# Running sums later, the weight sum T1 stored once, one statistics segment per batch, and the last batch's routing moved into the second phase's first rows

## The reference

```python
h = x @ base_weight.T + base_bias + (x @ A.T) @ Bw.T      # A, Bw of the batch's lora id
query = h @ Wq.T                                          # 2048 -> 64
scores = (query @ Wr.T) @ (aux_keys @ Wr.T).T / sqrt(48) + log_rel
top_scores, top_idx = top_k(scores, 8)                    # 8 of 512 slots
attn = einsum(query, aux_keys[top_idx]) / sqrt(64) + log_rel[top_idx]
w = softmax(attn)
aux = (w @ aux_values[top_idx]) @ Wvd.T @ Wvu.T
log_var = log1p(var(h, axis=-1))
learned = gelu(h @ Wu1.T + bu1) @ Wu2.T + bu2             # 2048 -> 512 -> 1
u = clip(0.5 * log_var / mean(log_var) + 2.5 * sigmoid(learned), 0, 5)
gate = sigmoid(0.5 * clip((u - 0.5) / 1.5, 0, 1) - 1.0)   # 0 where below 0.05
out = x + h + gate * aux
```

## Time and profile before

| | |
|---|---|
| median of 3 runs | 1995.03 us (1994.07 to 2000.32) |
| profiled execution | 1995.2 us, span 1993.4 us |
| PE busy | 1943.9 us (98%), mean granted clock 0.989 |
| DVE busy | 1262.0 us (63%) |
| ACT busy | 693.7 us (35%) |
| POOL busy | 400.9 us (20%) |
| DMA | 414.46 MB, mean 208 GB/s |

### The profile page before, as it was taken

The page is one execution under the profiler, slowest core; times in us unless marked ns, Lnnn a source line. Parts: engine busy times, 40 slices in busy tenths (PEclk is TensorE's granted clock), DMA queues, the critical chain, the costliest instruction groups (busy, mean ns, idle before and its releaser), DMA issues.

```text
span 1993.4 us, 24866 instructions
## 1 busy us (share of the span) xinstructions
PE 1943.9 (98%) x8682; PEld 1582.2 (79%) x8682; DVE 1262.0 (63%) x1656; ACT 693.7 (35%) x1051; POOL 400.9 (20%) x283
## 2 busy tenths in 40 slices
PE   8999999999999999999999999999999999999996
PEld 6877877888888888888888877777888888888875
DVE  5775688555467836546873643677377677667666
ACT  3422433333233433324333322344233323332332
POOL 2210122120022202002210100110433323233323
PEclk9989999999999999999999999999999999999997
DMA  7656777552367745146764434757977677777774
GB/s 268 229 190 244 254 252 258 168 173 74 131 202 232 225 147 187 45 154 210 234 208 140 159 106 171 240 184 236 326 269 270 231 244 236 229 241 237 274 275 164
DMA packets 195201, 414.46 MB, mean 208 GB/s; under 512 B 26692, under 2 KB 27716, under 8 KB 194950
## 3 DMA queue, kind: packets, MB, share of 16 engines
q1 hardware_dynamic: 150150, 324.78, 50.3%
q10 hardware_dynamic: 44928, 88.10, 11.5%
HBM read 316.32 MB, written 96.47 MB: 207 GB/s over the span
## 4 chain that ended last, share of the span: by engine, by line
PE 86%; DVE 7%; issue 3%; ACT 2%; DMA 2%; ACTq 0%; SPq 0%; DVEq 0%; POOL 0%; POOLq 0%
PE bank L1659 17%; PE bank L1660 17%; PE bank L1661 17%; PE bank L1697 6%; PE bank L1698 6%; PE bank L1699 6%; PE bank L1712 1%; PE bank L1713 1%; PE bank L1599 1%; PE bank L1600 1%; PE bank L1786 1%; PE bank L1788 1%; PE bank L1787 1%; DVE sums L1261 1%; PE bank L1767 1%
## 5 line engine op out<-in xcount | busy, mean ns | idle before, releaser
L1659 PE MATMUL bank<-xop,wsp 128*128 128x512 f32 x1792 | 710.7, 397 | 14.9 <-DVE wsp L1152 8.0
L1660 PE MATMUL bank<-xop,wsp 128*128 128x512 f32 x1792 | 701.8, 392 | 0.0
L1661 PE MATMUL bank<-xop,wsp 128*128 128x512 f32 x1792 | 700.9, 391 | 0.0
L1659 PEld LDWEIGHTS bank<-xop,wsp 128*128 128x128 f32 x1792 | 338.5, 189 | 98.6 <-DVE xop L1152 8.0
L1660 PEld LDWEIGHTS bank<-xop,wsp 128*128 128x128 f32 x1792 | 338.9, 189 | 74.5 <-issue 3.8
L1661 PEld LDWEIGHTS bank<-xop,wsp 128*128 128x128 f32 x1792 | 338.2, 189 | 72.4
L1152 DVE TENSOR_TENSOR wsp<-wraw,wsp 128x1024 fp32r<-128x1024 f32 x184 | 241.2, 1311 | 122.0 <-ACT wsp L790 121.7
L790 ACT ACTIVATE wsp<-wraw 128x1024 fp32r<-128x1024 f32 x184 | 194.0, 1054 | 204.3 <-PE bank L1661 170.9
L779 POOL TENSOR_TENSOR r_h<-r_h,r_x 128x512 f32<-128x512 f32 x128 | 172.7, 1349 | 363.7 <-DMA r_h<-h_dram 363.7
L877 ACT ACTIVATE stage<-stage 128x512 f32<-128x512 f32 x128 | 80.9, 632 | 406.1 <-DVE stage L1247 405.7
L1261 DVE TENSOR_TENSOR sums<-sums,stage 128x1024 f32<-128x1024 f32 x116 | 154.5, 1332 | 92.2 <-ACT stage L877 92.2
(11 more groups left out here) (158 smaller groups left out, 1957.9 us busy)
## 6 DMA issues: line engine op xcount, KB each, us to landing
wraw<-in_w SPq DMA_DIRECT2D x131, 512.0 KB, 3.8
xraw<-in_x SPq DMA_DIRECT2D x248, 256.0 KB, 4.2
wraw<-t_dram SPq DMA_DIRECT2D x80, 512.0 KB, 3.6
h_dram<-stage ACTq DMA_DIRECT2D x128, 256.0 KB, 3.9
hraw<-h_dram SPq DMA_DIRECT2D x128, 256.0 KB, 4.0
r_x<-in_x SPq DMA_DIRECT2D x128, 256.0 KB, 4.4
r_h<-h_dram SPq DMA_DIRECT2D x128, 256.0 KB, 3.5
out<-o_st ACTq DMA_DIRECT2D x96, 256.0 KB, 3.8
```

The costliest lines, as they stand in the source:

```text
L1659: pe.matmul(ps, wsp[:, slot, 0, f], x_hi(i), start=(k == 0), stop=False)
L1660: pe.matmul(ps, wsp[:, slot, 0, f], x_lo(i), start=False, stop=False)
L1661: last = pe.matmul(ps, wsp[:, slot, 1, f], x_hi(i), start=False, stop=(k == HT - 1))
```

## The change

- `add_sums(g - 2)` stands at the end of the iteration, in front of `finish(g - 1)`.
- The sums are kept per batch: two segments per pair, so 8 passes in place of 12; the last is in step 5 of phase 2. What uses the statistics moves from steps 4 to 9 to steps 7 to 14.
- ACT stores T1 from `t_res` in the iteration after it was made (`store_t1`); T2 waits until that has landed (`t_moved`). `make_t1_again` is gone, and M5 of pair 0 loads T1 from `t_dram` as the other pairs do. T4 is made beside tiles 16 to 23 (18 to 25 before).
- Batch 7 (`EARLY`): in row 0 of phase 2 ACT and DVE split its h from `r_h` before POOL adds x, and PE makes its query there with a lag of two steps. In rows 1 to 4 its four token tiles pass through scores, attention, selection and softmax, one per row in steps 14 and 15 (`SEQ` is the order of all of them). The normalised weights go to `a7_dram` and come back in row 7. At the end only the gate is multiplied in (`gated`).
- Selection has one DVE operation fewer per token tile, for all batches: MATCH_REPLACE writes 1e30, and one operation subtracts it and adds the attention.
- The end: 9 of batch 6's output blocks are added by DVE (`add_last6`), 7 are evacuated by ACT and added by POOL, in the order `TAIL6`; SP's stores of the two batches alternate.

```diff
         T1_AT = dict(zip((1, 2, 3, 4, 5, 6, 9, 11), range(HT)))
         T2_AT = dict(zip((8, 10, 12, 13, 14, 15, 16, 17), range(HT)))
-        T4_AT = {18 + o: o for o in range(HT)}
+        T4_AT = {16 + o: o for o in range(HT)}
         T3_AT = {M7 * HT - 3 + o: o for o in range(HT)}
-        T1B_AT = {M5 * HT - 3 + o: o for o in range(HT)}
...
-            early = p == 0 and q in (M7, M5)
+            early = p == 0 and q == M7
...
-        SEGMENT = {M2: 0, M4: 1, M5: 1, M3: 2}
-        STATS_AT = {(M6, 1): 0, (M3, 2): 1, (M1, 2): 2}
+        STATS_AT = {(M3, 3): 0, (M1, 3): -1}
+
+        def segment(p, q):
+            return 2 * p + (q in (M2, M3))
+
+        def segment_of_batch(b):
+            return b ^ 1
+
+        def stats_at(p, q, o):
+            seg = 2 * p + STATS_AT[q, o] if (q, o) in STATS_AT else -1
+            return seg if seg >= 0 else None
...
+        EARLY = NB - 1
+        SEQ = []
+        for b in range(NB - 1):
+            SEQ += [(b, t) for t in range(TT)] + ([(EARLY, b)] if b < TT else [])
+        POS = {bt: n for n, bt in enumerate(SEQ)}
+        QSEQ = [0, EARLY] + list(range(1, NB - 1))
+        QPOS = {b: n for n, b in enumerate(QSEQ)}
+        Q7_LAG = 2
+
+        def early_tile(c):
+            return c - 1 if 1 <= c <= TT else None
...
+        BY_DVE = 9
+        TAIL6 = (0, 1, 9, 10, 11, 2, 12, 3, 13, 4, 14, 15, 5, 6, 7, 8)
+
+        def aux_count(a):
+            b, o = a // KT, a % KT
+            return NAUX + TAIL6.index(o) + 1 if b == NB - 2 else a + 1
 
         def aux_place(a):
             b, o = a // KT, a % KT
             if b < NB - 2:
                 return aux_bank
             if b == NB - 2:
-                return (aux_bank, q_ps)[o % 2]
-            return (u_ps[2], u_ps[3], u_ps[0], u_ps[1])[o % 4]
+                return (aux_bank, q_ps)[o % 2] if o < BY_DVE else (u_ps[2], u_ps[3])[(o - BY_DVE) % 2]
+            return (aux_bank, q_ps, u_ps[2], u_ps[3])[o % 4]
+
+        def evacuated(j):
+            return r_x[:, j, :] if j < 4 else r_h[:, j - 4, :]
...
-                    b, o = NB - 2 + n // KT, n % KT
+                    b, o = NB - 1 - n // KT, n % KT
...
+            for o in range(BY_DVE):
+                store6(o)
+            for o in range(0, KT, 2):
+                store7(o)
+                store7(o + 1)
+                if BY_DVE + o // 2 < KT:
+                    store6(BY_DVE + o // 2)
...
+            def store_t1(o):
+                act.wait_ge(t_ready, t_count("t1", o))
+                act.dma_start(t_dram[T1, o], t_res[:, o, :]).then_inc(t_moved[o], 16)
...
+                if g - 1 in T1_AT:
+                    store_t1(T1_AT[g - 1])
...
+            def h7_hi(n):
+                act.wait_ge(rxh_in[n % 4], 32 * (n // 4 + 1))
+                wait(act, h7_used, n - 1)
+                to_hi(h7_sp[n % 2][:, 0, :], r_h[:, n % 4, :]).then_inc(h7h_ready, 1)
...
+            def store_a7(t):
+                act.wait_ge(wgt_ready, POS[EARLY, t] + 1)
+                act.dma_start(a7_dram[t], att7[:]).then_inc(a7_out, 16)
...
             def make_t2(o):
                 wait_w(dve, "t2", o)
-                dve.wait_ge(t_ready, t_count("t1", o))
+                dve.wait_ge(t_moved[o], 32)
...
-            def make_t1_again(o):
-                g = M5 * HT + o
...
-                if g > 1 and tile_of(g - 2)[1] in H_PRODUCTS:
-                    add_sums(g - 2)
...
-                if g in T1B_AT:
-                    make_t1_again(T1B_AT[g])
...
+                if g > 1 and tile_of(g - 2)[1] in H_PRODUCTS:
+                    add_sums(g - 2)
...
+                dve.match_replace(rep[:, n % 2, :], top8[:, n % 2, :], s_ps[:], CHOSEN).then_inc(sel_step, 1)
...
+                dve.scalar_tensor_tensor(tile, rep[:, n % 2, :], CHOSEN, s_ps[:], SUB, ADD).then_inc(msk_step, 1)
...
+            def gated(t):
+                dve.wait_ge(a7_in, 16 * TT)
+                dve.wait_ge(gate_step, GATE_STEPS * NB)
+                dve.tensor_scalar(att[:, t, :], att[:, t, :], gt[:, EARLY % 2, t:t + 1], None, MULT).then_inc(wgt_ready, 1)
...
+            def query7_pass(k):
+                pe.wait_ge(h7l_ready, k + 1)
+                if k == 0:
+                    pe.wait_ge(ax2_ready, NPAIR)
+                pe.matmul(aux_bank[:], wq_sp[:, k, :], h7_sp[k % 2][:, 0, :], start=(k == 0), stop=False)
+                pe.matmul(aux_bank[:], wq_sp[:, k, :], h7_sp[k % 2][:, 1, :], start=False, stop=(k == KT - 1))\
+                    .then_inc(h7_used, 1)
...
-                elif k == 1:
-                    stats_pass(3 * NPAIR - 1)
-                elif k == 8:
+                        score_pass(POS[b, SCORE_AT[k]])
+                    if k == KT - 2 and early_tile(c) is not None:
+                        score_pass(POS[EARLY, early_tile(c)])
+                elif k == 5:
+                    stats_pass(NB - 1)
+                elif k == 13:
                     pe.wait_ge(mstep, 5)
                     pe.matmul(mean_ps, ones[:], rowsum[:], start=True, stop=True).then_inc(mean_done, 1)
+                if 0 <= step - Q7_LAG < KT:
+                    query7_pass(step - Q7_LAG)
                 u_pass(step)
-                if k == 1:
+                if k == 1 and c < EARLY:
                     query_pass(step - 1)
-                if k > 0:
+                if k > 0 and c < EARLY:
                     query_pass(step)
                 if c >= 1 and k in SCORE_AT:
-                    attention_pass(b * TT + SCORE_AT[k])
+                    attention_pass(POS[b, SCORE_AT[k]])
+                if k == KT - 2 and early_tile(c) is not None:
...
             b, i = NB - 1, (NB - 1) * TT
             add_out(NAUX - 1)
-            query_sum(b)
+            add_last6(0)
             gelu_sum(b, 0)
             gelu_sum(b, 1)
-            query_lo(b)
+            add_last6(1)
             gelu_sum(b, 2)
             gelu_sum(b, 3)
-            selected(i)
-            selected(i + 1)
-            masked(i)
-            selected(i + 2)
-            masked(i + 1)
+            add_last6(2)
+            clipped(b)
+            add_last6(3)
             gate(b)
-            normalise(i)
-            selected(i + 3)
-            masked(i + 2)
-            normalise(i + 1)
-            masked(i + 3)
+            for t in range(TT):
+                gated(t)
+            add_last6(4)
             wt_lo(i)
-            normalise(i + 2)
             wt_lo(i + 1)
-            normalise(i + 3)
+            add_last6(5)
             wt_lo(i + 2)
+            wt_lo(i + 3)
             z_lo(b, 0)
-            wt_lo(i + 3)
+            add_last6(6)
             z_lo(b, 1)
+            add_last6(7)
+            add_last6(8)
             for o in range(KT):
-                add_last(o)
+                add_last7(o)
...
             b, i, a = NB - 1, (NB - 1) * TT, NAUX
-            aux_pass(a)
-            aux_pass(a + 1)
+            for o in TAIL6[0:4]:
+                aux_pass(a + o)
+            learned_pass(b)
+            for o in TAIL6[4:12]:
+                aux_pass(a + o)
             for t in range(TT):
-                score_pass(i + t)
-            learned_pass(b)
-            for t in range(TT):
-                attention_pass(i + t)
-                if t > 0:
-                    aux_pass(a + 1 + t)
-            aux_pass(a + 5)
-            turn_pass(i)
-            aux_pass(a + 6)
-            turn_pass(i + 1)
-            aux_pass(a + 7)
-            turn_pass(i + 2)
+                turn_pass(i + t)
+            aux_pass(a + TAIL6[12])
             z_pass(b, 0)
-            aux_pass(a + 8)
-            turn_pass(i + 3)
-            aux_pass(a + 9)
+            aux_pass(a + TAIL6[13])
             z_pass(b, 1)
-            for o in range(10, 2 * KT):
-                aux_pass(a + o)
+            aux_pass(a + TAIL6[14])
+            aux_pass(a + TAIL6[15])
+            for o in range(KT):
+                aux_pass(a + KT + o)
 
 
 # ---- launch: one core; kernel() lays the arrays out and launches ----
```

408 lines of the change are left out of this document (233 added, 175 removed).

## The result

The changed kernel takes 2022.55 us (median of four runs, 2017.99 to 2026.16) against 1995.62 us: 1.0127 times the time before, 95% interval 1.0104 to 1.0150. I had forecast 1986.4 us. It is 27 us slower, outside the range of 1962 to 2003. Its profiled execution spans 2024.2 us, 30.8 more than before.

What follows compares the result with a forecast made beforehand. TensorE (PE) was taken as the bound, 1943.9 of 1993.4 us. The terms summed to -8.8 us against the profiled 1995.2 us, giving 1986.4 us; own range 1978 to 1996, with rivals 1962 to 2003.

Steps and rivals of the forecast that it cites:

- Running sums later, in M5: In M5 of each pair, late DVE rounds grow by 0.97 us and PE waits for u_t: 3.0 us per pair.
- The collisions: DVE operations slowed beside POOL, as often as before: M5's late-sum cost 3.8 us per pair instead of 3.0, 2.0 without any.
- T1 made once: M4 and M5 of pair 0: eight DVE adds of 1.22 us and their waits go, 10.3 us less.
- The stores: T1's eight 512 KB stores move to M1, issued by ACT: +0.5 us, between 0 and +3.
- Pair 0, M2 to M7: DVE-bound stretch of pair 0: x later by 3.9 us, weight buffers and clock added, +7.5; M7 -0.4.
- the ring: Three weight buffers in pair 0: T4(0) before T2(7) waits for store and load, 6.2 us, 2.9 not beside rounds.
- Statistics: Four of twelve passes in PE's stream go, -7.4 us; with M6's wait of 0.3, -7.7.
- The door and phase 2: Between phases: last finish later, last sum's wait gone, +3.5 us; moved batch 7 matmuls in rows 1 to 4, +3.6.
- Row 0: Phase 2's first row: forecast 0 us; rival, chance 0.08: query 7's r late, 1 us per step, 2002 us.
- The end: Last u matmul to batch 7's first output pass: +22.5 us instead of +41.6, so -19.1; additions and stores behind it +1.6.
- hidden: Rival, chance 0.22 wholly or by half: late sums cost nothing in DVE's rounds; 1951 us, half of it 1969.
- The clock rival: Chance 0.12: new waits in M5 lower PE's clock once or twice per pair, 1.7 us each, +13.6: 2000 us.

Runs made afterwards that it cites:

- e1: The changed kernel with the running sums back in their old place, in front of the low half of the weights: 1981.14 us, ratio 0.9931.
- e4: The changed kernel with POOL's phase 1 additions cut to 64 of 512 columns: 1985.44 us, ratio 0.9958.
- e8: e1 with POOL's phase 1 additions cut to 64 of 512 columns: 1970.52 us, ratio 0.9882.
- e9: e7 without the eight T1 stores, M5 reading a raw quarter of w instead: 1963.19 us, ratio 0.9838.
- e7: e3 with T4 made beside tiles 18 to 25 again: 1970.45 us, ratio 0.9871.
- e5: e1 with T4 made beside tiles 18 to 25 again: 1973.01 us, ratio 0.9897.
- e2: The kernel before with one edit, the running sums right in front of finish: 2066.55 us, ratio 1.0364.
- e3: The changed kernel with the sum of one tile later (g-3) behind the finish, where DVE waits for ACT: 1971.30 us, ratio 0.9879.
- e6: The kernel before with the sum of one tile later in the wait behind the finish, and three statistics passes one tile later: 1987.44 us, ratio 0.9960.

## Why the prediction was wrong

Its sum was -8.8 us, the span grew by 30.8. By its own steps:

- **Running sums later, in M5: +12 for four pairs was taken, +39 came.** This is the step that failed. From M4 to M3 of the pairs the changed kernel loses 11.4, 8.2 and 8.5 us in pairs 1 to 3, and in pair 0 +0.7 where e1, with the old place, has -10.3, so 11.0. The rule that I stepped by was right: the low half starts 2.75 after the finish, a bare round takes 5.04 (from 676.48 to 681.52 in M5), PE waits for finish plus 1.49. Without collisions the term was not too small either: 4.8 us for four pairs (e4 against e8), where I had 2.0 per pair. The round's length was wrong: I took rounds of M4 as 5.05 plus splits and put a collision only where one had stood before. In the changed kernel the sum met POOL in four rounds of M4, pair 1 (three adds of 2.29 to 2.31 us instead of 1.23 and a copy of 1.79 instead of 0.69), and the low half in two. The lag at the door of M5 was 7.8 and not 4.2, and M5 then runs with a lag of 4.7 to 6.0 in six of its other seven tiles, and each stretch from one lora matmul to the next is 0.5 to 1.8 us longer than 5.69. Of the 39 us, 27 are waits for u_t, 7 the lower clock (1.7 us once per pair) and the rest is not broken down.
- **The collisions were nearly dismissed.** I gave them 1.0 us per pair (3.0 instead of 2.0), at most 1.8; by e4 and e8 they are 34.3 of the 39.1 us in this stretch, 8.6 per pair. This is the rule of the Trainium skill (GPSIMD Engine Reference, Key points) that GpSimd and VectorE contend for SBUF when VectorE has two operands there; the trace agrees (1.78 us against 0.69), and I should have kept it at full weight. But "as often as before" did not hold where it mattered: from M4 to M3 of pairs 1 to 3 DVE spent 14.6 us beyond its usual durations before and 26.5 after. What I had not seen either is that the old order hid its collisions: a finish that waits for PE absorbs a 1.1 us operation, a finish that DVE is late for passes it on. Even the 3.8 us per pair that I gave to that case was too small, since it counted collisions in M5 and not those in M4 that fill the lag.
- **T1 made once, -10.3: right.** In e1 M4 to M3 of pair 0 is 10.3 us shorter, the same number. The stores were taken for +0.5, at most +3, and are some 4 by the profiled executions of e9 and e7.
- **Pair 0, M2 to M7: +7.1 taken, +5.0 with M6's statistics pass counted; +10.2 came.** e1 and e5 divide it, from M2's start to M4's: late sums 5.8 (10.2 against 4.4), the ring 9.7 (4.4 against -5.3). The clock is in both: I took 0.7 for it, and the mean granted clock of the stretch is 0.94 where it was 0.97, some 5 us (an estimate from these two). I priced T4's place by one load behind one store, 2.9 us, and for M7 put -0.4; in truth the loop of 9 us per T4 stood two turns longer in front of x.
- **Statistics, -7.7: right.** Each pair from 1 on starts M4 1.85 us earlier against the line before it. What I did not see is that this edit also takes the passes away from late sums (e2: 18.5 us of waits).
- **The door and phase 2: +7.1 taken, +9.6 came, but this stage is the uncertain one (e9).** The wait for the last finish was not 8.1 but 3.9 and 1.5 us, the sum's wait of 3.0 went. Four waits for the gelus at rows' starts (2.2 us), where the query matmuls of the step before no longer stand in front of u, and one of 1.3 for h were not in my sum. Row 0 was not starved.
- **The end: -17.5 taken (-19.1 and +1.6), -14.1 came.** The first output pass stands 25.5 us behind the last u matmul, inside my 20.6 to 26, and two waits of 2.1 and 1.4 us for DVE, of which the first is for the weighted sums of the gelus, are why it isn't 22.5.

The rivals: "hidden" was wrong for the changed kernel. The clock rival, about 2000, had the right place and a right part: waits in M5 of every pair, and behind them one stretch of low clock per pair at 1.7 us, as it said for "once or twice". That is 7 of the 39 us; the waits themselves are the larger part. The mean granted clock of the whole execution, 0.988 against 0.989, hides this, since from the last u matmul to the end it was 0.82 before and is 0.92 now. My lowest chance was on the side that came. The price of the late sums had its upper bound from one pair's rows as they stood (3.8 us per pair); the same rows with the sums beside POOL too, 1.1 us more in such a round, would have given far more, and that end I did not work out.

## What to carry to other kernels

An operation that waits in an engine's queue for another engine isn't freed by moving it later: ask what the engine does in the wait that is left. Here the same sum cost 39 us more at the end of the round than in its old place (the changed kernel against e1). In the gap behind the finish, where DVE had to wait in any case, it was 10 us better than in the old place in one pair of kernels (e3 against e1), 8 in another (e6 against the kernel before), and not to be told from it in a third (e7 against e5).

When a loop is close to the pace of the engine that it serves, count the worst case of each of its operations, not the usual one: as long as there is slack at its end collisions are free (0 us from M4 to M3 in e1 against e8), and they are paid from the round on in which the slack is gone (34 us in the changed kernel against e4).

A table that says beside which tile a thing is made is also a position in a ring and in another engine's queue; multiply by the ring's own turn (9 us here), not by the tile's (5.5).
